# Two queues for the first batch, results stored in halves, the router as the held operand, gathers and scatters that wait for data alone

## The reference

```
x = x + 0.5 * ffn(layernorm(x))
x = x + attn(layernorm(x))
x = x + 0.5 * ffn(layernorm(x))

ffn(x):  shared   = (silu(x @ sgate.T) * (x @ sup.T)) @ sdown.T        # 256 hidden units
         probs    = sigmoid(x @ router.T + routing_bias)               # 8 experts
         scores, indices = top_k(probs, 2);  scores /= sum(scores)
         combined = sum over the two experts e of  score * (silu(x@gate_w[e]) * (x@up_w[e])) @ down_w[e]
         return shared + combined
attn(x): q, k, v, gate projections; rotary q and k; 8 heads of 16; linear attention in the form
         (scale * q @ (k^T v) + sum v) / (scale * q . sum k + S);
         plus a 5-tap depthwise convolution of v; times gate; output projection
```

## Time and profile before

| | us |
|---|---|
| median of 3 runs | 469.5 (469.5 to 469.87) |
| profiled execution, its own time | 470.26 |
| its span, first to last instruction | 468.5 |

### The profile page before, as it was taken

The page is one execution under the profiler, slowest core; times in us unless marked ns, Lnnn a source line. Parts: engine busy times, 40 slices in busy tenths (PEclk is TensorE's granted clock), DMA queues, the critical chain, the costliest instruction groups (busy, mean ns, idle before and its releaser), DMA issues.

```text
span 468.5 us, 9695 instructions
## 1 busy us (share of the span) xinstructions
PE 443.2 (95%) x2959; PEld 377.1 (80%) x2959; DVE 353.5 (75%) x1112; ACT 265.1 (57%) x596; POOL 281.6 (60%) x290
## 2 busy tenths in 40 slices
PE   7999999999999999999899999998899999999992
PEld 3878878888889888879787788887779888887872
DVE  4899996333688978999899999998899743454553
ACT  5965145555766657667533675654285565565630
POOL 4127556777775067713878850777574767763771
PEclk9999999999999999999999999999899999999998
DMA  7991143355422334311113321221443445553332
GB/s 225 366 341 46 55 127 123 99 174 135 127 84 83 92 95 112 109 44 52 57 53 90 96 70 51 69 80 63 124 129 104 135 148 148 152 160 102 95 102 63
DMA packets 74210, 53.62 MB, mean 114 GB/s; under 512 B 9648, under 2 KB 68784, under 8 KB 74160
## 3 DMA queue, kind: packets, MB, share of 16 engines
q1 hardware_dynamic: 65968, 36.19, 26.1%
q0 software_dynamic: 8192, 16.79, 12.1%
HBM read 26.81 MB, written 26.15 MB: 113 GB/s over the span
## 4 chain that ended last, share of the span: by engine, by line
PE 49%; DVE 22%; POOL 12%; issue 8%; DMA 4%; ACT 3%; SPq 0%; POOLq 0%; DVEq 0%; ACTq 0%
PE pool L899 13%; POOL x_sorted L1150 6%; PE gu L847 6%; PE pool L888 6%; PE gu L849 6%; PE gu L848 6%; POOL yg L1170 4%; PE pool L830 3%; DVE X L1236 2%; DVE hs L1213 2%; DVE hs L1217 2%; DVE stats L1247 2%; PE gu L806 1%; ACT xn L1059 1%; DVE xt_lo L1269 1%
## 5 line engine op out<-in xcount | busy, mean ns | idle before, releaser
L1150 POOL DMA_INDIRECT x_sorted<-xn,places x128 | 130.0, 1016 | 64.1 <-issue 33.0
L1170 POOL DMA_INDIRECT yg<-y_sorted,places x128 | 123.7, 966 | 54.2 <-issue 35.7
L1036 ACT ACTIVATE gs<-gu 128x512 f32<-128x512 f32 x124 | 72.4, 584 | 74.3 <-PE gu L849 37.6
L1213 DVE TENSOR_TENSOR hs<-gs,gu 128x512 f32<-128x512 f32 x92 | 60.6, 663 | 59.3 <-ACT gs L1036 58.4
L899 PE MATMUL pool<-w,hT 128*128 x708 | 96.9, 281 | 0.1
L899 PEld LDWEIGHTS pool<-w,hT 128*128 128x128 f32 x708 | 87.4, 191 | 11.3 <-issue 7.7
L847 PE MATMUL gu<-w,xbt_hi 128*128 x177 | 82.4, 465 | 1.5 <-DVE hs L1217 0.9
L849 PE MATMUL gu<-w,xbt_hi 128*128 x177 | 70.3, 397 | 0.0
L848 PE MATMUL gu<-w,xbt_lo 128*128 x177 | 70.2, 396 | 0.0
L1042 ACT ACTIVATE hT<-pool 128x512 f32<-128x512 f32 x92 | 53.3, 581 | 24.0 <-PE pool L888 22.7
L1017 ACT ACTIVATE ys<-pool 128x256 f32<-128x256 f32 x92 | 34.5, 375 | 46.8 <-PE pool L899 46.5
(11 more groups left out here) (137 smaller groups left out, 765.4 us busy)
## 6 DMA issues: line engine op xcount, KB each, us to landing
xb<-x_sorted SPq DMA_DIRECT2D x85, 128.0 KB, 2.4
y_sorted<-ys SPq DMA_DIRECT2D x85, 128.0 KB
x_sorted<-yg SPq DMA_DIRECT2D x6, 512.0 KB, 7.7
X<-x_dram SPq DMA_DIRECT2D x8, 256.0 KB, 4.6
x_sorted<-xn,places POOLq DMA_INDIRECT x128, 2.3
yg<-y_sorted,places POOLq DMA_INDIRECT x128, 2.7
out_dram<-X SPq DMA_DIRECT2D x8, 256.0 KB
raw<-gate_w_dram SPq DMA_DIRECT2D x4, 256.0 KB, 4.9
```

The lines of the kernel that those rows point to most:

```text
L1036: nc.scalar.activation(dst, src, ACT.Silu).then_inc(silu_done, 1)
L1150: nc.gpsimd.indirect_dma_start(x_sorted[g], bass.IndirectOffsetOnAxis(places[g][:, k, t:t + 1], 0), xn[:, b, t % T], None).then_inc(scatte ...
L1170: nc.gpsimd.indirect_dma_start(yg[slot][:, k, t], None, y_sorted[g], bass.IndirectOffsetOnAxis(places[g][:, k, at:at + 1], 0)).then_inc(ga ...
L1213: v.tensor_tensor(hs[n % HB][:].rearrange("p (j i) -> p j i", j=2)[:, 0:k], gs[n % GB][:].rearrange("p (j i) -> p j i", j=2)[:, 0:k], bank ...
```

## The change

1. **First batch by two queues.** SP loads tiles 0 and 1 of batch 0, ScalarE's queue tiles 2 and 3. VectorE normalizes the latter two (`norm_rest`), while ScalarE does the former. In the order of loads the shared gate and up matrices come ahead of the tables, and the shared down matrix has its own semaphore.
2. **Router held.** `logits` takes the router as the stationary operand, with zero columns ahead of it (`MARGIN`) so that the results of the members of a group fall on different partitions, and streams 512 tokens: two matmuls for each pass. ScalarE adds the bias while it copies 16 rows of 512 out of PSUM. For each group TensorE turns the rows (`logit_turn`, 4 transposes), and VectorE adds the high and low halves (`halves`, one reduction for each member).
3. **Fronts start on the high part.** Expert and shared units, and the attention projections, run the two products with the high part first and wait for the low part before the third.
4. **No pace.** `through` and `pace` are gone; gathers and scatters wait for their data and buffers alone.
5. **Adds and results in halves.** The gathers for the first and for the second expert have their own semaphores. The last of a pass's three adds signals after half its tiles, and SP stores each half by itself.
6. **Order.** Lengths in the plan are new, and so is the string of priorities.

```
-        op(("stats", l, b), "DVE", 80, *needs, ("moments", l, b - 1) if b else None)
+        op(("stats", l, b), "DVE", 80, *needs, ("moments", l, b - 1) if b else None,
+           ("norm_rest", 1, 0) if (l, b) == (1, 1) else None)
...
+            sp.dma_start(X[:, 0, 0:2], x[0].rearrange("(t p) d -> p t d", p=P)[:, 0:2]).then_inc(x_loaded[0], 16)
...
+            act.dma_start(X[:, 0, 2:4], x[0].rearrange("(t p) d -> p t d", p=P)[:, 2:4]).then_inc(x_rest_loaded, 16)
...
+            def norm_rest(l, b):
+                once.wait_ge(shift_done[l], b + 1)
+                for t in (2, 3):
+                    ins = v.tensor_scalar(xn[:, b, t], X[:, b, t], rstd[:, l, b, t:t + 1], shifts[:, l, b, t:t + 1],
+                                          ALU.mult, ALU.add)
+                ins.then_inc(norm_rest_done, 1)
...
+                row, i = ROWS * GROUPS[group_of(l, b)].index((l, b)), plan.xt_of[l, b]
+                pe.matmul(pool_ps[m][0:row + 2 * E], router_cut[:, MARGIN - row:], xt_hi[i][:], start=True, stop=False)
+                pe.matmul(pool_ps[m][0:row + E], router_cut[:, MARGIN - row:MARGIN + E], xt_lo[i][:],
+                          start=False, stop=True).then_inc(logits_ready[l], 1)
+
+            def logit_turn(g):
+                for l, b in GROUPS[g]:
+                    once.wait_ge(logits_read[l], b + 1)
+                once.wait_ge(squares_loaded, 16)
+                m = plan.misc["logit_turn", g]
+                take(m, halves_done, g + 1)
+                n = ROWS * len(GROUPS[g])
                 for t in range(T):
+                    mm = pe.transpose(pool_ps[m][:, t * P:t * P + n], logit_rows[0:n, t * P:(t + 1) * P], ident[0:n, 0:n])
...
-                    pe.matmul(dst[:, 2 * t * E:2 * (t + 1) * E], hi[:, at],
-                              router_cut[:].rearrange("p r e -> p (r e)"), start=True, stop=False)
-                    mm = pe.matmul(dst[:, 2 * t * E:(2 * t + 1) * E], lo[:, at], router_cut[:, 0], start=False, stop=True)
...
+                rows = slice(row, row + 2 * E)
+                nc.scalar.activation(logit_rows[rows], misc("logits", l, b)[rows], ACT.Identity,
+                                     bias=bias_rows[rows, 0:1]).then_inc(logits_read[l], 1)
...
+            def halves(g):
+                once.wait_ge(logits_turned, g + 1)
...
+                parts = misc("logit_turn", g)[:].rearrange("p (t i r) -> p t i r", t=T, r=ROWS)
+                for i in range(len(GROUPS[g])):
+                    ins = v.tensor_reduce(L[g][:, i * T:(i + 1) * T],
+                                          parts[:, :, i, 0:2 * E].rearrange("p t (r e) -> p t e r", r=2), AX.X, ALU.add)
+                ins.then_inc(halves_done, 1)
...
-                    once.wait_ge(xbt_lo_done, r + 1)
...
-                    pe.matmul(dst[:, j], xbt_lo[r % 2][:, at], hi, start=False, stop=False)
-                    mm = pe.matmul(dst[:, j], xbt_hi[r % 2][:, at], lo, start=False, stop=True)
+                    pe.matmul(dst[:, j], xbt_hi[r % 2][:, at], lo, start=False, stop=False)
+                    once.wait_ge(xbt_lo_done, r + 1)
+                    mm = pe.matmul(dst[:, j], xbt_lo[r % 2][:, at], hi, start=False, stop=True)
...
-                half_through, through = plan.through(key)
-                wait(once, half_ready, half_through)
-                wait(once, gu_ready, through)
...
-                pace("scatter", g, n)
...
-                pace("gather", l, b, n)
...
-                if k == 0:
-                    once.wait_ge(gathered[b], 16 * 2 * T * (1 if l == 1 else 2))
-                    once.wait_ge(weigh_link, 3 * (g + 1))
+                once.wait_ge(gathered[b][k], 16 * T * (1 if l == 1 else 2))
+                once.wait_ge(weigh_link, 3 * (g + 1))
...
+                    if t == T - 1 or (t == 1 and update(l, b, step) == LAST):
+                        ins.then_inc(updated[b], 1)
...
+                for h in range(2):
+                    once.wait_ge(updated[b], LAST + h)
+                    half = slice(2 * h, 2 * h + 2)
+                    sp.dma_start(out[b].rearrange("(t p) d -> p t d", p=P)[:, half], X[:, b, half]).then_inc(stored, 16)
```

More of the change, by code:

```diff
@@ L142, in describe @@
             self.shared(3, b)
-            op(("out", b), "SP", 47, *(("add", 3, b, s) for s in ("first", "second", "shared")))
+            op(("out", b), "SP", 94, *(("add", 3, b, s) for s in ("first", "second", "shared")))
         for g in range(NG):
@@ L167, in norm @@
         if l != 2:
-            op(("logits", l, b), "PE", 90, ("lo", l, b), ("cut_router_lo",))
-            op(("bias", l, b), "DVE", 33, ("logits", l, b), ("tables",))
+            op(("logits", l, b), "PE", 47, ("lo", l, b), ("cut_router_lo",))
+            g = group_of(l, b)
+            op(("bias", l, b), "ACT", 58, ("logits", l, b), ("router",), ("logit_turn", g - 1) if g else None)
     def shared(self, l, b):
@@ L192, in route @@
         op = self.op
[L193 to L197, removed]
-        op(("clamp", g), "DVE", 32, *logits, ("weigh", g - 1) if g else None)
+        op(("logit_turn", g), "PE", 45, *(("bias", *member) for member in GROUPS[g]))
+        op(("halves", g), "DVE", 17 * len(GROUPS[g]), ("logit_turn", g), ("tables",), ("probs", g - 2) if g >= 2 else None)
+        op(("clamp", g), "DVE", 32, ("halves", g), ("weigh", g - 1) if g else None)
         op(("sigmoid", g), "ACT", 31, ("clamp", g))
         op(("inverse", g), "DVE", 47, ("clamp", g))
-        op(("probs", g), "DVE", 92, ("inverse", g), ("sigmoid", g))
-        op(("best", g), "DVE", 116, ("probs", g))
-        op(("second", g), "DVE", 142, ("best", g))
+        op(("probs", g), "DVE", 104, ("inverse", g), ("sigmoid", g))
+        op(("best", g), "DVE", 120, ("probs", g))
+        op(("second", g), "DVE", 150, ("best", g))
         op(("choose", g), "DVE", 13, ("second", g))
@@ L216, in route @@
         for n in range(2 * tiles(g)):
-            op(("scatter", g, n), "POOL", 126, ("place", g), *free, ("norm", *GROUPS[g][n // 2 // T], 1), lands=200)
+            op(("scatter", g, n), "POOL", 126, ("place", g), *free, ("turn", *GROUPS[g][n // 2 // T]), lands=200)
             free = (("scatter", g, n),)
@@ L226, in experts @@
                 done = [("gather", l, b, n)]
-            op(("add", l, b, "first"), "DVE", 106, ("gather", l, b, 2 * T - 1), ("weigh", g))
-            op(("add", l, b, "second"), "DVE", 106, ("add", l, b, "first"))
+            op(("add", l, b, "first"), "DVE", 106, ("gather", l, b, T - 1), ("weigh", g))
+            op(("add", l, b, "second"), "DVE", 106, ("add", l, b, "first"), ("gather", l, b, 2 * T - 1))
     def routed(self, r, g, n):
@@ L332, in stage @@
         return group_of(1, b) + 0.5 if l == 2 else group_of(l, b)
-    ROUTING = ("clamp", "sigmoid", "inverse", "probs", "best", "second", "choose", "count", "based", "place", "table",
+    ROUTING = ("logit_turn", "halves", "clamp", "sigmoid", "inverse", "probs", "best", "second", "choose", "count", "based", "place", "table",
                "weigh")
@@ L517, in schedule @@
         return True
-    def through(self, key):
-        t = self.start[key]
-        return tuple(sum(1 for u in self.units if self.end.get(("front", u, j), t) + HOP <= t) for j in (1, 0))
 def build(nc, x, wk, wv, wq, wg, wo, lepe_w, lepe_b, sgate, sup, sdown, gate_w, up_w, down_w,
@@ L696, in update, with through @@
             return (0 if l == 1 else 4) + done.index(step) + 1
+        def through(l, b, step):
+            n = update(l, b, step)
+            return LAST + 1 if n == LAST else n
         def freed(n):
@@ L905, in shared_down @@
                 once.wait_ge(h_done, nth_hidden["S", l, b, 1] + 1)
+                once.wait_ge(shared_down_loaded, 16)
                 m = plan.misc["sdown", l, b]
-                take(m, updated[b], update(l, b, "shared"))
+                take(m, updated[b], through(l, b, "shared"))
                 for t in range(T):
@@ L998, in _ @@
             multiply_ones(0, WARM)
[L999 removed]
+            run("PE", {"turn": xn_turn, "logits": logits, "logit_turn": logit_turn, "count": count, "regs": find_experts, "pair_turn": pair_turn,
                        "front": front, "hidden_turn": hidden_turn, "down": down, "sdown": shared_down, "kv": kv,
@@ L1163, in gather @@
                     if old:
-                        once.wait_ge(updated[old[1]], update(*old, "second"))
+                        once.wait_ge(updated[old[1]], through(*old, "second"))
                     elif slot == YG - 1:
```

229 lines of the change are left out of this document (123 added, 106 removed).

## The result

The changed kernel takes 457.07 us (median; 456.09 to 458.57) beside 469.69 us of the kernel before on the same chip: a ratio of 0.9732, 95% interval 0.9702 to 0.9761, so 12.6 us less. The forecast was 463.4: the side was right, the size half of what came. The range (456.5 to 470.0) held it, and the rival *gaps closed* had 457.4, but not by the mechanism that happened, as the experiments show. Where the text sets one kernel's profile beside another's, each is of one execution.

The account below looks back on a forecast made before the run. TensorE was taken to set the pace alone from 62 to 130 us, VectorE being as full before 62 and from 210 to 265; terms summed to -6.1 off 469.5, giving 463.4, range 456.5 to 470.0.

Parts of the forecast that it names:

- gaps closed: Rival: the new order also removes half the idle time and clock loss, 7 us instead of 1: 457.4; chance 0.18.
- Order: Whole kernel: new engine order wins a small -1.0 us, bounded by 16.8 of TensorE idle ahead of the tail plus 1.7 clock.
- Router: Routing in all 16 passes: net -3.2 us on TensorE, about half counted, -1.5; ends 0 and -3.2.
- routing becomes the bound: Rival: four hand-overs ahead of `clamp` cost 3.0 us a group; with three groups slower, 473.4; chance 0.14.
- Head: Kernel start: sooner first turn, half-batch landing and first shared front, -1.5 us; ends 0 and -3.4.
- Tail: Kernel end: four adds fewer after the last landing, -1.15, and a half-size last store, -0.45: -1.6 us.
- No pace: Gathers and scatters without waits for TensorE's progress: -0.5 us; ends 0 and -2.0; the 7.36 scatter wait not real.
- High part: Expert fronts starting on the high part: 0 us; ends 0 and -1.5.
- three signs by which I wanted to be wrong: Places of groups 0, 3 or 4 over a microsecond later; new clock drops; last group's first gather no sooner than 449.24.

Follow-up runs that it names:

- after_onequeue: The changed kernel with both halves of the first batch issued by SyncE, one after the other: ratio 0.9731 to the kernel before.
- before_nopace: The kernel before without the waits of gathers and scatters for TensorE's progress, nothing else changed: ratio 0.9969, -1.5 us.

## Why the prediction was wrong

**Order (-1.0): the step that failed.** "I take a small gain", out of bounds of 18.5 either way. It measured -3.4 on the old parts and -14.7 on the changed ones. The bounds held both; two things were wrong inside them. The gain was taken as small for want of a row, not because a row spoke for it. And I priced the order as a part beside the others, while it is what decides their prices: the same router and head cost 3.7 us (1.0046 against 0.9968) in one order and bring 5.0 (0.9838 to 0.9732) in the other. Step by step, the order brought 3.4, the pace, high part and halves 4.2 more in it, router and head 5.0 more, where the forecast had 1.0, 2.1 and 3.0. Why the old order turns the new router into waiting is open beyond the delays shown above. The idle time, from which the bounds were taken, also shows too little of the waiting: a matmul that is in flight longer while the next waits counts as busy there. Ahead of the last matmul, which starts 13.6 us sooner, the idle time fell by 3.9, the work by 5.2 and the waiting by 8.4.

**Router (-1.5):** half of the work saved was counted, and about that or less was measured in both orders. The work saved was more than the 3.2 forecast: 5.3, with the head. The rival *routing becomes the bound* had a mechanism that the old order shows: there the changed kernel is slower than before (1.0046), with places 2.7 to 3.1 us later in groups 0, 3 and 4, near its price of 3.0 for a group. The searched order hides it, which neither rival nor forecast provided for.

**Head (-1.5): nothing to be seen by 102 us; no run has it alone.** The sooner turn (8.22) and front (11.33) came; the three engines' new steps then met on ScalarE (the logits' step at 11.90, the cut, the table load). Under the router I had cost "ScalarE gains a 512-column step" at nothing, with its share of 57% as cover; at the head that cover isn't there. after_onequeue and the changed kernel have the same ratio (0.9731 and 0.9732). The Trainium skill ("DMA: Bandwidth & Descriptors", Issuing engines are not separate DMA queues) says that DMAs started by several engines run on the same DMA engines, and that starting them on several saves only the time to issue; the two ratios agree with that.

**Tail (-1.6): 0 by the profiles** (10.39 us from the last gather to the end, before and after). The steps happened (four adds, 1.13), but on a chain that didn't end last. I had followed the chain of waits to the last add and store; it ended at 465.7, and GpSimd's drain at 468.2.

**No pace (-0.5):** -1.5 (-2.2 to -0.7) in the old order, inside its bounds. The reading that 7.36 before the scatter at 217.69 wasn't real is borne out (217.9 in before_nopace). **High part (0):** 0, with the halves, in the old order.

*Gaps closed* (457.4) had the number and not the way: idle time ahead of the last matmul fell by 3.9 (16.8 to 12.9), not by 7. Its own sum was off as well: half of 16.8 and 1.7 is 9.2, not 7, and would have made 455.2. Two of the three signs by which I wanted to be wrong came (group 0's places 2.4 later, a new clock drop in the head), and the kernel was faster all the same: with another order group 0's lateness costs nothing by 102 us.

## What to carry to other kernels

When a change brings parts and a new order at once, price the order on the new parts, and test it by two transplants: the parts in the old order, the order with the old parts. A change of a wait without a new order can cost far more than the wait (36 us here). Before a tail is shortened, look at the closing rows of every engine, and see whose drain ends last.

## What the runs showed of the hardware

GpSimd's closing drain lasts 9.22 us beyond its last indirect gather in 18 of the 20 profiles here, with no DMA moving in the last 4.5 us of the changed kernel; leaving out the last four gathers (1.25 us each, 5.0) took 5.5 us off the time. ScalarE loads a table of 1.28 us twice, at its first copy and at its first Silu (1.23 and 13.87 in the changed kernel); with a small Silu ahead of all (after_silu) there is one.
